# Activating the later u and q projections of an attention and FP4 feed-forward layer on VectorE, 256 tokens per tile, in place of ScalarE

## What is computed

```python
x_proj = jax.nn.silu(x @ W1 + b1)
u, v, q, k = jnp.split(x_proj, 4, axis=-1)
scores = jnp.einsum('bqhd,bkhd->bhqk', qh, kh)
attn = jax.nn.silu(scores) / S
av = jnp.einsum('bhqk,bkhd->bqhd', attn, vh).reshape(B, S, D)
y = _layernorm(av * u, gamma, beta) @ W2 + b2
x = _layernorm(x + y)
# feed-forward, every operand quantised to FP4 in blocks of 16
gate = fp4_linear(x, w_gate)
h = jax.nn.silu(gate) * fp4_linear(x, w_up)
x = _layernorm(x + fp4_linear(h, w_down))
```

## Time and profile before

| what | value |
|---|---|
| median of 3 runs | 516.97 us (515.13 to 518.89) |
| the profiled execution's own time | 516.72 us |
| its span | 514.9 us |
| mean granted TensorE clock | 0.995 of full speed |
| ScalarE busy | 487.4 us, 95% |
| TensorE busy, matmuls | 495.3 us, 96% |
| TensorE busy, weight loads | 262.5 us, 51% |
| VectorE busy | 282.1 us, 55% |
| GpSimd busy | 78.6 us, 15% |

### The profile page before, as it was taken

How to read it: one execution, slowest core, us unless ns; L and a number is a source line. 1 busy time by engine, 2 the same in 40 slices (tenths; PEclk the granted TensorE clock), 3 DMA queues, 4 the chain that set the end, 5 groups by cost and what they waited for, 6 DMA issues and landing times.

```text
span 514.9 us, 20166 instructions
## 1 busy us (share of the span) xinstructions
PE 495.3 (96%) x9030; PEld 262.5 (51%) x9032; DVE 282.1 (55%) x723; ACT 487.4 (95%) x547; POOL 78.6 (15%) x176
## 2 busy tenths in 40 slices
PE   7799999999999999999999999999999999999996
PEld 4354334444344444434344444444477877777762
DVE  6446641665848375573947366583844433435445
ACT  4899999999999999999999999999999999999940
POOL 7600000102020200202020110202020202112010
PEclk9899999999999999999999999999999999999999
DMA  7932340000000000000000000000000000000000
GB/s 188 210 91 52 106 127 20 1 3 6 3 6 3 7 3 3 7 1 8 1 8 4 5 4 1 8 1 9 3 8 4 9 4 10 4 8 10 4 3 12
DMA packets 15157, 12.40 MB, mean 24 GB/s; under 512 B 1783, under 2 KB 14718, under 8 KB 15070
## 3 DMA queue, kind: packets, MB, share of 16 engines
q1 hardware_dynamic: 14088, 9.44, 7.3%
q0 software_dynamic: 688, 1.40, 1.1%
q10 hardware_dynamic: 294, 0.26, 0.2%
HBM read 1.92 MB, written 1.05 MB: 6 GB/s over the span
## 4 chain that ended last, share of the span: by engine, by line
ACT 48%; PE 30%; issue 16%; DVE 2%; DMA 2%; POOL 0%; SPq 0%; POOLq 0%; DVEq 0%
ACT attn L650 48%; PE ps L412 28%; PE ps L426 2%; DMA x_sb<-in_L_attn_x 1%; DMA k_stack<-parts 1%; ACT feat L650 0%; POOL rstd_b L384 0%; DVE xn_b L776 0%; DVE stats_b L806 0%; DVE xn_b L780 0%; SPq L286 0%; DVE xn_b L782 0%; DVE xn_b L784 0%; DVE parts L754 0%; DVE feat L751 0%
## 5 line engine op out<-in xcount | busy, mean ns | idle before, releaser
L650 ACT ACTIVATE attn<-ps 128x1024 f32<-128x1024 f32 x512 | 475.6, 1210 | 2.2 <-PE ps L412 1.9
L412 PE MATMUL ps<-attn,v_pad 128*32 128x256 f32 (+1 forms) x5120 | 275.2, 342 | 0.3 <-DVE wdown_t L991 0.2
L412 PE MATMUL ps<-q_stack,k_stack 64*128 64x256 bf16 (+1 forms) x2560 | 173.8, 251 | 10.9 <-ACT attn L650 1.4
L412 PEld LDWEIGHTS ps<-attn,v_pad 128*32 128x32 f32 x5120 | 132.4, 109 | 80.8 <-issue 40.3
L412 PEld LDWEIGHTS ps<-q_stack,k_stack 64*128 64x128 bf16 x2560 | 78.8, 94 | 134.3 <-ACT attn L650 85.7
L383 POOL TENSOR_TENSOR ve_a<-mv_a,eps_col 128x1 f32<-128x1 f32 x24 | 4.6, 192 | 212.4 <-DVE mv_a L808 212.4
L383 POOL TENSOR_TENSOR ve_b<-mv_b,eps_col 128x1 f32<-128x1 f32 x24 | 4.6, 192 | 194.6 <-DVE mv_b L808 194.6
L749 DVE CAST parts<-feat 128x512 bf16<-128x512 f32 (+1 forms) x10 | 3.9, 390 | 26.7 <-ACT feat L650 26.7
L384 POOL TENSOR_TENSOR rstd_a<-ve_a,minus_half 128x1 f32<-128x1 f32 x24 | 13.5, 562 | 1.9
L384 POOL TENSOR_TENSOR rstd_b<-ve_b,minus_half 128x1 f32<-128x1 f32 x24 | 13.5, 561 | 1.9
L412 PE MATMUL ps<-zeros 128*128 128x512 bf16 x46 | 12.2, 412 | 1.4 <-DVE zeros L928 1.2
(11 more groups left out here) (185 smaller groups left out, 404.1 us busy)
## 6 DMA issues: line engine op xcount, KB each, us to landing
q_stack<-parts SPq DMA_DIRECT2D x18, 128.0 KB, 2.4
k_stack<-parts SPq DMA_DIRECT2D x15, 128.0 KB, 3.9
x_sb<-in_L_attn_x SPq DMA_DIRECT2D x3, 256.0 KB, 6.4
k_stack<-zeros SPq DMA_DIRECT2D x6, 128.0 KB, 5.4
q_stack<-zeros SPq DMA_DIRECT2D x6, 128.0 KB, 2.4
k_stack<-parts SPq DMA_DIRECT2D x9, 64.0 KB, 2.5
q_stack<-parts SPq DMA_DIRECT2D x9, 64.0 KB, 2.0
out<-x_a SPq DMA_DIRECT2D x8, 64.0 KB, 1.6
```

Source lines behind the costliest of these rows:

```text
L412: return pe.matmul(to, lhsT, rhs, start=start, stop=stop, skip_group_check=True)
L650: return act.activation(to, frm, ACT.Silu, **kw)
```

## The change

For q from token 1024 on and u from token 512 on, ten pieces of 256 tokens in all, the projection leaves chunk 0 and becomes a job "late" in the wide chunks, one per tile 0 to 9, at step 5 (even tile) or 21 (odd tile) of the chunk. VectorE does the SiLU in ScalarE's place, in four parts between its stages: `late_read` (bias added, out of PSUM) after the y stage, `late_exponent` after the xqT copy, `late_sum` after the quantising of h, and `late_product` (reciprocal and product, for q also the split) after the hqT copies. The buffers are those of the other tile's rows. q pieces go with tiles 0, 2, 4 and 6, u pieces with tiles 1, 3, 5, 7, 8 and 9. SyncE stacks each late q ahead of the output of its tile.

```diff
-               15: ("u", 1), 17: ("q", 512), 19: ("u", 2), 21: ("q", 1024), 23: ("u", 3), 25: ("q", 1536),
-               27: ("w2", 0), 29: ("gate", 0), 31: ("up", 0), 33: ("down", 0)}
+               17: ("q", 512), 27: ("w2", 0), 29: ("gate", 0), 31: ("up", 0), 33: ("down", 0)}
...
+    LATE = {0: ("q", 1024), 1: ("u", 512), 2: ("q", 1280), 3: ("u", 768), 4: ("q", 1536),
+            5: ("u", 1024), 6: ("q", 1792), 7: ("u", 1280), 8: ("u", 1536), 9: ("u", 1792)}
+    LW = 256
+    LATE_AT = {t: BEGIN[t // 2 + 1] + (21 if t % 2 else 5) for t in LATE}
     JOB_AT = {at: (kind, i, None) for at, (kind, i) in PREP_AT.items()}
+    JOB_AT |= {at: ("late", 0, t) for t, at in LATE_AT.items()}
...
             for n in range(KT):
+                if n in LATE and LATE[n] in unit_no:
+                    stack(sp, unit_no[LATE[n]])
                 sp.wait_ge(x2_ready, n + 1)
...
+                if kind == "late":
+                    last = project(bank, *LATE[tile], LW)
...
+            def late_read(tile):
+                x, n, f, spare = late_buffers(tile)
+                col = 0 if LATE[tile][0] == "u" else 1
+                bank = wait_made("late", 0, tile)
+                dve.tensor_scalar(x, ps[:, bank, 0:LW], b1_col[:, col:col + 1], X_MIN,
+                                  ALU.add, ALU.max).then_inc(job_by_vec, 1)
+                wait_taken("late", 0, tile)
+
+            def late_exponent(tile):
+                x, n, f, spare = late_buffers(tile)
+                link(dve.tensor_scalar(n, x, -LOG2_E, Y_MIN, ALU.mult, ALU.max))
+                link(dve.tensor_scalar(spare, n, ROUND, None, ALU.add))
+                link(dve.scalar_tensor_tensor(out=f, in0=spare, scalar=ROUND, in1=n,
+                                              op0=ALU.subtract, op1=ALU.subtract))
+                link(dve.tensor_scalar(n.bitcast(U32), spare.bitcast(U32), 23, None, ALU.logical_shift_left))
+                link(dve.scalar_tensor_tensor(out=spare, in0=f, scalar=POWERS[4] / LAST, in1=f, op0=ALU.add, op1=ALU.mult))
+
+            def late_sum(tile):
+                x, n, f, spare = late_buffers(tile)
+                for power in (3, 2, 1):
+                    link(dve.scalar_tensor_tensor(out=spare, in0=spare, scalar=POWERS[power] / LAST, in1=f,
+                                                  op0=ALU.add, op1=ALU.mult))
+                link(dve.scalar_tensor_tensor(out=spare, in0=spare, scalar=POWERS[0] / LAST, in1=n,
+                                              op0=ALU.add, op1=ALU.mult))
+                link(dve.tensor_scalar(spare, spare, LAST, 1.0, ALU.mult, ALU.add))
+
+            def late_product(tile):
+                x, n, f, spare = late_buffers(tile)
+                kind, start = LATE[tile]
+                link(dve.reciprocal(f, spare))
+                if kind == "u":
+                    link(dve.tensor_tensor(uT[:, start:start + LW], x, f, ALU.mult))
+                else:
+                    link(dve.tensor_tensor(feat[:, unit_no[LATE[tile]] % FEAT, 0:LW], x, f, ALU.mult))
+                    split(kind, start)
...
             fp4(Blocks(blocks, blocks, P, NBF, ROWS[0]), wq_ready)
-            split("q", 1024)
-            split("q", 1536)
...
                 if kind == "y":
                     to_quantised_x(tile)
+                elif kind == "late":
+                    late_read(tile)
                 elif kind == "xqT":
                     copy_xqT(tile)
+                    if tile in LATE:
+                        late_exponent(tile)
...
                     gated_h(tile)
+                    late_sum(tile)
...
                     copy_hqT(tile)
+                    if tile in LATE:
+                        late_product(tile)
```

More of the change, by code:

```diff
@@ L30 @@
 Y_MAX, Y_MIN = 120.0, -125.0
+X_MIN = -Y_MAX / LOG2_E
 POWERS = (1.00000007, -0.69314697, 0.2402212, -0.05550713, 0.00967554, -0.00132765)
@@ L132, in build @@
     UNITS = [("k", 0, 256), ("q", 0, 256), ("k", 256, 512), ("k", 768, 512), ("k", 1280, 512), ("k", 1792, 256),
-             ("q", 256, 256), ("q", 512, 512), ("q", 1024, 512), ("q", 1536, 512)]
+             ("q", 256, 256), ("q", 512, 512)]
+    UNITS += [(*unit, LW) for unit in LATE.values() if unit[0] == "q"]
     unit_no = {unit[:2]: n for n, unit in enumerate(UNITS)}
@@ L305, in _ @@
                 zero_rows(sp, n)
-                stack(sp, n)
+            for start in (256, 512):
+                stack(sp, unit_no[("q", start)])
             for n in range(KT):
+                if n in LATE and LATE[n] in unit_no:
+                    stack(sp, unit_no[LATE[n]])
                 sp.wait_ge(x2_ready, n + 1)
@@ L545, in job @@
                     pe.wait_ge(av_taken, STEPS[at - LAG][0])
-                if tile is not None:
+                if kind == "late":
+                    last = project(bank, *LATE[tile], LW)
+                elif tile is not None:
                     last = behind(kind, tile, bank)
@@ L743, in split @@
                     dve.wait_ge(head_act, head_no[(kind, start)] + 1)
-                else:
+                elif (kind, start) not in LATE.values():
                     dve.wait_ge(job_by_act, ACT_JOBS.index(job_no[(kind, start, None)]) + 1)
@@ L890, in activate_gate, with late_buffers @@
                 link(dve.reciprocal(f, spare))
+            def late_buffers(tile):
+                o = ROWS[(tile + 1) % 2]
+                return (o.gate[:, 0:LW], o.magic[:, 0:LW], o.xn[:, 0:LW],
+                        o.hqT[:, :, :].rearrange("p t n -> p (t n)")[:, 0:LW])
+            def late_read(tile):
[5 more added lines that the diff above has]
+                wait_taken("late", 0, tile)
```

## The result

| | before | changed |
|---|---|---|
| median of 22 runs each | 516.72 us | 518.36 us |
| ratio, 95% interval | | 1.004 (1.0027 to 1.0053) |
| span of the profiled execution | 514.9 us | 517.2 us |

The change costs about 2 us, 0.4%: slower, but by under a third of the 6.9 us (1.3%) that I forecast. That is within 1%, the case to which I gave 0.39.

The account below looks back on a forecast made before the run. The prediction took ScalarE to bound the kernel, with TensorE's slack at the odd boundary some 0.03 us. It summed 516.72 - 2.9 + 6.2 + 3.6 = 523.6 us, 1.3% slower, range 517 to 528.

Parts of the forecast that it names:

- The bound and the gain: ScalarE sets the time; five 512-column activations leaving chunk 0 save 0.57 us each, 2.9 us gained.
- The cost is where the work stands, not how much it is: VectorE's added 74 us fit its 40% free time by sum, but by place not everywhere.
- read the other way as in the prediction: Rival that VectorE, at 60%, can take the work and only the gain shows: 513.8 us; chance 0.12.
- The late job at 0: Late projection on TensorE, two bare steps behind a boundary: 0.57 us, just fits, cost 0.
- the reciprocal at 1.75: VectorE's reciprocal of 256 columns in late_product, taken as 1.75 us from the line between 22 and 352 columns.
- The odd boundary: Tiles 1, 3, 5, 7, 9: late take_av delays down and scores, 1.0 us at tile 9, 1.3 at others, 6.2 in all.
- the carry: Lateness that an even tile's q piece passes to the next odd boundary, 0.3 us at tiles 1, 3, 5 and 7.
- The even boundary: Tiles 0, 2, 4, 6 with a q piece: ScalarE loses 0.9 us each, 3.6 us in all.
- Its first term: Even boundary with q: read of down moves 1.1 us, so y waits and ScalarE stalls 0.35 us.
- the stall of the scores behind xqT: Even boundary with q: later quantised x and late_read delay xqT, so the scores behind it cost another 0.26 us.
- the third term: Even boundary with q: the scores after gate come at 186.88 against 186.58, another 0.3 us.
- only take_av binds: Rival: even-boundary cost and carry vanish, leaving 5 x 1.0 us at odd boundaries; 518.8 us, chance 0.17.

Follow-up runs that it names:

- e1: Changed kernel with late_product of the odd tiles moved behind take_av; 515.21 us, ratio to the kernel before 0.9983, span 512.0.
- e2: Changed kernel without the reciprocal of the late pieces, the product taken with its argument; span 511.9 us.
- e5: As e1, with the second half of a late q's split behind the statistics of down; 514.36 us, ratio to the kernel before 0.9961.
- e10: The kernel of e5 a second time; 512.87 us, ratio to the kernel before 0.9955.
- e4: Changed kernel with only the u pieces late, q from 1024 on back in chunk 0 in pieces of 512; span 515.7 us.
- e8: Kernel before with two scratch reciprocals of 256 columns between the hqT copies and take_av of the odd tiles; span 523.7 us.
- e9: As e1, but late_read of the odd tiles reads 8 columns in place of 256; 299.99 us from activation 64 to 391.
- e3: Changed kernel with a second reciprocal of 256 columns in late_product of the odd tiles; span 525.8 us.
- e6: Changed kernel with only the q pieces late, u back in chunk 0 in pieces of 512; span 513.7 us.
- e7: Kernel before with one scratch reciprocal of 256 columns between the hqT copies and take_av of the odd tiles; span 516.4 us.

## Why the prediction was wrong

*The bound and the gain: right.* ScalarE sets the time, and the five 512-column jobs of chunk 0 were worth 0.57 us each by the forecast; 2.80 us of 2.9 came.

*"The cost is where the work stands, not how much it is": right.* Both places named are where ScalarE waits, and e1 and e2 take the waits away with all of the late projections left in. By the rule of the Trainium skill (Perfetto Trace Analysis, section "Optimizing Scalar/DVE Operations"), read the other way as in the prediction, the time would have been 513.8. The changed kernel did not reach that; e5 and e10 show that the free time was there, once the order was right.

*The late job at 0 and the reciprocal at 1.75: right,* by e2 and by the 1.74 us in the profile.

*The odd boundary, 1.0 and 1.3 us: too high,* 0.62 and 0.82 to 0.84, in all 3.9 us and not 6.2. Two terms were mis-sized. First, the delay of down: 0.79 us without and 1.02 with the carry (e4, changed kernel), where I had 1.0 and 1.3. I had put every new instruction 0.035 us behind the one before. That holds for linked instructions; one that does not wait for its predecessor starts 0.08 us before that one's end (the reciprocal at 140.25, the copy until 140.33; and in the same way the first step of late_sum at 137.55, the end of the quantising at 137.63). The carry was 0.22, not 0.3. Second, I let the whole delay of down pass on to the scores. In truth 0.16 us of it is swallowed, since the stretch from down's first weights to the next scores shrinks (0.983 us in the trace of before, 0.824 in that of the changed kernel). e8 shows the same at a delay of 1.89. Why it shrinks I read from the rows as follows, without having tested it: TensorE's matmuls of attn x v are still running when down is issued undisturbed, and down's weights queue behind them; after a wait that work is done.

*The even boundary, 0.9 us: the step that failed most,* 0.07 to 0.17 and once 0.53, in all 0.9 us and not 3.6. Its first term, 0.35 us of waiting of y, is nothing: the read of down came 0.6 us late and not 1.1, by the same early starts (0.08 at the reciprocal and again at the read of down, each counted as a gap of 0.035 instead), casts of 0.294, and the copies 0.25 instead of 0.4 late; y did not move at all at any of the four, and by the rows it would have moved only beyond some 0.7 (an estimate: the read ends at 175.23 before the change, and y loads its weights at 176.02). With that, the stall of the scores behind xqT (0.26) goes too: xqT is 0.56 to 0.66 us late at tiles 0, 2 and 6, its own stretch shrinks from 0.54 to 0.36, and 0.61 of slack was there. Only the third term is left, half of it. Four small errors, all in one direction, each added to a threshold: since a wait begins only where slack ends, 0.1 us too much in a chain becomes 0.1 us too much in every tile. Tile 4's 0.53 is another thing: an instruction of VectorE's chain (the aggregate of the statistics) started 0.35 us later than in its neighbours, and the late projection, which may not start before y's bank has been read, waited for x1p. That dependence was missing in the prediction. In e1, e5, e9 and e10 a delay of that size stood at tile 2, at another instruction, and none at tile 4. What makes these delays is open, so of the 0.9 us of the even boundaries some 0.35 are not explained.

*The range and the sign.* Slower was right, and the median lies inside the range of 517 to 528. But 1.3% was wrong: it is 0.4%. The sum was a difference of a sure small gain and nine uncertain losses that all hung on the same few hundredths of slack; I should have let the range of each term, not its middle, decide the likeliest case. Of the recorded rivals "only take_av binds" (518.8) came closest, and it had most of the mechanism: y does not move, and the even boundary costs little. It left out the carry, which e4 shows (0.22 us), and priced the odd boundary at 1.0, so that its number is right in part because two errors offset each other (5.0 in its sum, 3.9 + 0.9 measured).

## What to carry to other kernels

Free time of an engine is worth something only at the place where the work stands: ask for every inserted group which instruction behind it somebody is waiting for, and put it behind that one. Here two instructions moved behind take_av and two more behind the read of down turned 0.4% slower into 0.4% faster, at the same amount of work. When a cost is a delay beyond a slack, take the starts of unlinked instructions, and what shrinks behind a wait, from rows of the trace before adding up.

## What was not expected of the hardware

- TensorE's clock fell from 1.00 to 0.50 of full speed behind a wait of about 2.9 us in e3, at one of five boundaries alike, and was back within about 4 us; it cost 1.5 us. At the other four boundaries of e3, three of them with a wait as long, it stayed at 1.00, and so it did with the waits of 1.7 to 2.0 us in e8's profile.
- The start of the program has two lengths. Profiles of before, of the changed kernel, e2, e4, e5, e6, e7, e8 and e9 have a wait of ScalarE of 1.2 to 1.6 us behind the sixth activation; in e1, e3 and e10 it is absent. Windows from 10 to 30 us, before and e10:

```profile
10.00:30.00 20.00, 17.38 (x216) 9.43 (x216) 10.50 (x15) 16.67 (x22) 10.43 (x22) 0.91 0.88 207
```

```profile
10.00:30.00 20.00, 17.70 (x245) 9.72 (x244) 10.50 (x15) 18.36 (x24) 11.96 (x27) 1.00 0.84 210
```

The granted clock of that stretch is 0.91 where the wait is there and 1.00 where it is not. The fall comes first. In the profile of before TensorE waits for a DMA into k_stack until 17.75, and then its clock is at 0.50, 1.2 GHz:

```profile
18.00:20.00 2.00, 2.00 (x24) 0.86 (x24) 0.49 (x1) 2.00 (x3) 2.00 (x5) 0.50 1.15 221
```

In that stretch 16 matmuls of attn x v take 1.93 us (1.07 in e10), and the scores for which ScalarE waits load their weights only at 21.78. In e10 TensorE waits for the same DMA until 16.95 and keeps 1.00. Why some executions fall and others do not was not tested. The difference is as large as what this change is about, so single spans were compared only from activation 64 on.
- A reciprocal of 256 columns takes 1.74 us, four times a scalar_tensor_tensor of that width (0.42).
